# A two-layer attention block on one core: weighted values in three blocks a half instead of four

## The chip, the cores and the metric

The kernel runs on one NeuronCore of one Trainium2 chip. The metric is the device time of one execution in microseconds (us). The engines are named as in the profile: PE (TensorE, matmuls), DVE (VectorE), ACT (ScalarE), POOL (GpSimd) and SP (the queue that issues most transfers). PEld is the loading of weights into PE.

## What is computed

The input `x` is 8 images of 256 channels by 32 x 32 pixels, float32. Two attention layers follow each other; the second takes the first one's result. With `s = 1024` pixels and 8 heads of 32 channels, a layer is, cut to what matters:

```python
xn = group_norm(x, gamma, beta)                  # 32 groups of channels
qkv = einsum('bchw,oc->bohw', xn, w_qkv) + b_qkv
q, k, v = split(qkv per head)                    # 32 channels each
m = softmax(einsum('bhcs,bhct->bhst', q * scale, k * scale), axis=-1)
a = einsum('bhst,bhct->bhcs', m, v)
out = einsum('bchw,oc->bohw', a, w_proj) + b_proj
return x + out
```

## The kernel before, in words

The work is cut into 16 blocks (two layers of eight images), each into two groups of four heads. A block and a group are a **slot**; there are 32. In the code `s.g` is 0 for a block's first slot and 1 for its second. A slot has 64 **units** (`UNITS`), and falls into two **halves** of 32 units, one for each 512 queries. In a half there are 8 key tiles of 128 keys; unit `u` is one key tile and one of the four heads.

Every engine's program walks over the same units, in an order written out by numbers at the head of the file. In unit `u` PE does, in this order (`slot` of the PE program):

- `scores_t` (L398): 128 keys by 512 queries into one of three banks `ps_t`. ACT takes the exponential into a tile `pt` (L655).
- `dense` (L480, L488, L495): at two units of every eight, one part of a dense matmul into the single bank `ps_d`: queries and keys of two slots ahead (L480), values of the next block (L488), or the output projection of the block before (L495). Two parts make a step; its result is evacuated by ACT and DVE, or by DVE alone, one or two units later.
- `scores_for_max` (L425): scores with queries on the partitions, 40 units ahead, into one of three banks `ps_m`. DVE takes the row maxima (L737), and every eighth unit a small reduction over them (L746), which SP copies into row 96 of the queries.
- `sums` (L471): four matmuls with ones, once a half, that add up the exponentials of the half before over the partitions. They use a place in the ring of `ps_m`.
- `weighted_values` (L449): four matmuls of 32 columns for each key tile, side by side in the array, into `ps_v`.

What the ones-matmuls add up is made by POOL: `add` (L906) adds the key tiles of a half one by one, seven tiles in six additions of 128 x 2048, and `add_last_tile` (L913) starts a transfer that adds the eighth. `sums` waits for the landing:

```python
if t == ALL_BUT_LAST:
    pe.wait_ge(last_tile_added, 16 * (half + 1))
```

POOL's first addition of a half waits for the exponentials of its first two tiles, that is for unit 7. In the slots of group 0 POOL has `scale_and_shift` (L885 to L891) ahead of its additions: seven small operations on the statistics of the next block's group norm. They wait for `gm_done`, which ACT gives (L680) after PE's `group_stats` (L503). PE issues that at unit `GN_AT`. The next block's statistics are taken by DVE in the slots of group 1 (`channel_stats`, L771, at the units `STATS_AT`), and ACT normalises in the slots of group 0 at the units `NORMALISE_AT`.

When the sums of a half are there, DVE divides (`divide`: L784, L787, L790, L795). The attention result `att` of a half is what the output projection waits for. `values_out` (L663) copies `ps_v` away on ACT once the eighth tile of a half is in. A tile `pt` is one of six; an exponential waits until the tile six before it has been through `weighted_values` and through POOL's addition, or the transfer.

The last three halves are summed otherwise: POOL adds fewer tiles and PE's ones-matmuls take the rest, with no transfer.

## Time and profile before

| | us |
|---|---|
| median of 3 runs | 2068.94 (2068.49 to 2068.95) |
| the profiled execution | 2059.56 |
| its span | 2057.8 |
| PE busy | 2023.7 (98%) |
| POOL busy | 1838.2 (89%) |
| DVE busy | 1685.0 (82%) |
| ACT busy | 1248.9 (61%) |

The span is the time from the first to the last instruction in the profiled execution. Matmuls overlap in the pipeline, so PE's busy time says that it always had something, and the distance between starts is what a matmul costs. PE's granted clock is 0.997 of full speed on the mean. The run falls into a start of some 63 us, 32 slots, and an end of a few microseconds.

### The profile page before, as it was taken

The numbers are of one execution on the slowest core, as the hardware profiler recorded it, in microseconds if no ns is written. First come the engines' busy times: TensorE is split into PE (matmuls) and PEld (weight loads), VectorE is DVE, ScalarE is ACT, GpSimd is POOL, SyncE is SP. The second block draws the span as 40 slices with busy tenths as digits, with TensorE's granted clock in tenths as the row PEclk, the third lists the DMA queues.
The fourth block names the chain that finished last, engine by engine and source line by source line (L and its number), as shares of the span: only waits on it lengthen the run. The fifth ranks groups of instructions, "written<-read, shape, count | busy, mean of one in ns | idle before, by whom it ended". The sixth has DMA issues, their size and how long they took to land.

```text
span 2057.8 us, 30311 instructions
## 1 busy us (share of the span) xinstructions
PE 2023.7 (98%) x10080; PEld 1124.5 (55%) x10080; DVE 1685.0 (82%) x2896; ACT 1248.9 (61%) x2321; POOL 1838.2 (89%) x626
## 2 busy tenths in 40 slices
PE   6999999999999999999999999999999999999998
PEld 3455555655556555565555556555565555555543
DVE  5888888888888888888888888888888888888882
ACT  1556666666666666666566666666666666665664
POOL 2699999999899998999989999998999989999985
PEclk9999999999999999999999999999999999999999
DMA  4355455544456445366454555444564454654431
GB/s 129 73 112 105 92 113 124 119 104 96 107 110 144 100 90 120 83 143 144 102 107 86 123 124 121 106 94 109 107 144 103 88 118 85 143 123 83 105 60 42
DMA packets 217306, 220.31 MB, mean 107 GB/s; under 512 B 167488, under 2 KB 167616, under 8 KB 209344
## 3 DMA queue, kind: packets, MB, share of 16 engines
q1 hardware_dynamic: 207792, 152.84, 33.1%
q0 software_dynamic: 8784, 63.97, 15.9%
q10 hardware_dynamic: 576, 1.57, 0.4%
q8 instruction: 81, 1.33, 0.3%
q14 instruction: 73, 0.60, 0.1%
HBM read 36.32 MB, written 16.78 MB: 26 GB/s over the span
## 4 chain that ended last, share of the span: by engine, by line
PE 88%; DVE 6%; POOL 2%; DMA 2%; issue 1%; ACT 0%; SPq 0%; DVEq 0%; POOLq 0%; ACTq 0%
PE ps_t L398 23%; PE ps_m L425 21%; PE ps_v L449 20%; PE ps_d L480 10%; PE ps_d L495 5%; PE ps_d L488 5%; DVE raw_max L737 3%; PE ps_m L471 3%; POOL acc L906 2%; DMA acc<-pt 1%; DVE ps_m L790 1%; DVE att L795 1%; DVE turned L784 1%; DVE res L806 1%; PE ps_m L480 0%
## 5 line engine op out<-in xcount | busy, mean ns | idle before, releaser
L655 ACT ACTIVATE pt<-ps_t 128x512 f32<-128x512 f32 x2048 | 1122.1, 598 | 753.3 <-PE ps_t L398 728.6
L737 DVE TENSOR_REDUCE raw_max<-ps_m 128x1 f32<-128x512 f32 x2048 | 1332.5, 686 | 277.0 <-PE ps_m L425 275.3
L906 POOL TENSOR_TENSOR acc<-acc,pt 128x2048 f32<-128x2048 f32 x315 | 1442.4, 4579 | 45.1 <-ACT pt L655 1.4
L425 PE MATMUL ps_m<-ks,qs 96*128 96x512 f32 x2048 | 985.9, 482 | 8.3 <-DVE raw_max L737 6.0
L398 PE MATMUL ps_t<-qs,ks 97*128 97x512 f32 x2048 | 842.7, 413 | 1.3 <-ACT pt L655 1.1
L398 PEld LDWEIGHTS ps_t<-qs,ks 97*128 97x128 f32 x2048 | 389.5, 190 | 364.5 <-issue 216.1
L425 PEld LDWEIGHTS ps_m<-ks,qs 96*128 96x128 f32 x2048 | 388.6, 190 | 192.1 <-DVE raw_max L737 105.1
L449 PE MATMUL ps_v<-pt,v 128*32 128x512 f32 x4096 | 491.2, 597 | 0.0
L906 POOL TENSOR_TENSOR acc<-pt 128x2048 f32<-128x2048 f32 x64 | 300.3, 4692 | 61.4 <-ACT pt L655 60.3
L480 PE MATMUL ps_d<-xn,wq 128*128 128x512 f32 x500 | 256.9, 596 | 5.7 <-ACT xn L687 5.7
L449 PEld LDWEIGHTS ps_v<-pt,v 128*32 128x32 f32 x4096 | 113.9, 109 | 257.8 <-issue 187.4
L495 PE MATMUL ps_d<-att,wp 128*128 128x512 f32 x252 | 130.2, 597 | 4.7 <-DVE att L795 4.7
L488 PE MATMUL ps_d<-wq,xn 128*128 128x256 f32 x488 | 125.1, 378 | 0.0
L480 PEld LDWEIGHTS ps_d<-xn,wq 128*128 128x128 f32 x500 | 96.0, 192 | 30.1 <-issue 8.8
L488 PEld LDWEIGHTS ps_d<-wq,xn 128*128 128x128 f32 x488 | 92.2, 189 | 17.1
L913 POOL DMA_DIRECT2D acc<-pt x61 | 54.4, 892 | 34.1 <-ACT pt L655 33.6
L471 PE MATMUL ps_m<-acc,ones 128*32 128x512 f32 x512 | 68.1, 604 | 0.9 <-DMA acc<-pt 0.8
L784 DVE STREAM_TRANSPOSE turned<-ps_m 128x512 f32<-128x512 f32 x64 | 45.3, 708 | 27.7 <-PE ps_m L471 27.7
L495 PEld LDWEIGHTS ps_d<-att,wp 128*128 128x128 f32 x252 | 46.7, 190 | 21.5 <-issue 9.4
L674 ACT ACTIVATE stage_qh<-ps_d,par 128x512 fp32r<-128x512 f32 x63 | 43.0, 683 | 21.5 <-DMA ks<-stage_kh 13.8
L755 DVE SCALAR_TENSOR_TENSOR stage_ql<-ps_d,par,stage_qh 128x512 fp32r<-128x512 f32 x63 | 47.0, 746 | 9.5 <-ACT stage_qh L674 9.5
L806 DVE SCALAR_TENSOR_TENSOR res<-ps_d,bp,res 128x512 f32<-128x512 f32 x63 | 46.8, 743 | 9.2 <-PE ps_d L495 9.2
(50 smaller groups left out, 528.9 us busy)
## 6 DMA issues: line engine op xcount, KB each, us to landing
acc<-pt POOLq DMA_DIRECT2D x61, 1024.0 KB, 8.8
qs<-stage_qh SPq DMA_DIRECT2D x256, 128.0 KB, 2.4
ks<-stage_kh SPq DMA_DIRECT2D x248, 128.0 KB, 2.4
qs<-stage_ql SPq DMA_DIRECT2D x128, 128.0 KB, 2.5
qs<-neg_max SPq DMA_DIRECT2D x1024, 0.5 KB, 2.0
ks<-stage_kl SPq DMA_DIRECT2D x124, 128.0 KB, 2.4
xn<-x_dram SPq DMA_DIRECT2D x16, 512.0 KB, 4.5
res<-x_dram SPq DMA_DIRECT2D x16, 512.0 KB, 4.4
```

The source lines that it names most:

```text
L398: pe.matmul(ps_t[(UNITS * s.n + u) % RING][:, :], ks[s.qk][0:KROWS + 1, h, t * P:(t + 1) * P], qs[s.qk][0:KROWS + 1, h, hf * HALF:(hf + 1) ...
L425: pe.matmul(ps_m[place % RING][:, :], qs[b][0:KROWS, h, c:c + P], ks[b][0:KROWS, h, kf * HALF:(kf + 1) * HALF], start=True, stop=True).the ...
L449: mm = pe.matmul(ps_v[HD * h:HD * (h + 1), :], v[s.v][:, t, c:c + HD], tile_of(half, t)[:, h, :], start=(t == 0), stop=(t == NT - 1))
L471: mm = pe.matmul(ps_m[place % RING][HD * h:HD * (h + 1), :], ones[:, :], tile[:, h, :], start=first and k == 0, stop=last and k == len(til ...
L480: mm = pe.matmul(bank[:, :], wq[:, kt, c:c + P], xn[parity][:, kt, hf * HALF:(hf + 1) * HALF], start=(kt == 0), stop=(kt == CT - 1))
L488: mm = pe.matmul(bank[:, t * C:(t + 1) * C], xn[parity][:, kt, (2 * r + t) * P:(2 * r + t + 1) * P], wq[:, kt, 2 * C:3 * C], start=(kt == ...
L495: mm = pe.matmul(bank[:, :], wp[:, kt, ct * P:(ct + 1) * P], att[:, kt, hf * HALF:(hf + 1) * HALF], start=(kt == 0), stop=(kt == CT - 1))
L655: act.activation(tile_of(half, t)[:, h, :], ps_t[(UNITS * s.n + u) % RING][:, :], ACT.Exp, scale=SCALE).then_inc(exp_done, 1)
L737: dve.tensor_reduce(raw_max[:, e % 2, t, kf:kf + 1], ps_m[MAX_PLACE["max", UNITS * n + w] % RING][:, :], AX.X, ALU.max)\
L784: dve.transpose(turned[:, :], ps_m[bank][:, :]).then_inc(divide_step, 1)
L806: dve.scalar_tensor_tensor(out=r, in0=bank[:, :], scalar=bp[:, ct:ct + 1], in1=r, op0=ALU.add, op1=ALU.add).then_inc(proj_done, 1)
L906: pool.tensor_tensor(acc[hf][:, :, :], a[:, :, :], tile_of(half, t)[:, :, :], ALU.add).then_inc(pool_added, 1)
```

## The change

It sets the places anew at which things stand in a half. Only numbers and the code that reads them change.

- `weighted_values` stood at units 3, 11, 19 and 27 of a half, two key tiles each. Now it stands at unit 7 (the last two tiles of the half before), 17 (tiles 0 to 2) and 29 (tiles 3 to 5).
- A dense step's two parts stood three units apart, at the units 6 and 9 of every eight counted on (so 1, 6, 9, 14, 17, 22, 25 and 30 of a half). Now the four steps of a half stand at units 3 and 4, 11 and 16, 20 and 21, 26 and 27. No step reaches over into the next slot any more, so the code for that is gone.
- The ones-matmuls go from unit 19 to unit 17 of the next half, still ahead of the weighted values of that unit.
- The group statistics go from unit 7 to 9, the channel statistics from 39, 42, 44, 49 to 37, 39, 42, 44, the normalisation from 13, 17, 25, 29 to 17, 21, 25, 29, and `values_out` from unit 4 to unit 8.
- In the last three halves the sums go from unit 11 to 17, and the last slot's own places go up by one or two.

```diff
@@ -57,16 +57,17 @@
 LATER = 1
-PV_AT = 3
-PV_TILES = 2
-DENSE_AT = (6, 9)
-SUMS_AT = 19
-SUMS_AT_END = 11
+PV_BLOCKS = {7: (-2, -1), 17: (0, 1, 2), 29: (3, 4, 5)}
+LAST_TILES = 2
+VALUES_OUT_AT = 8
+DENSE_AT = ((3, 4), (11, 16), (20, 21), (26, 27))
+SUMS_AT = 17
+SUMS_AT_END = 17
 ROWS_AT = 7
 START_QK, START_LOW = 6, 2
-STATS_AT = (39, 42, 44, 49)
-GN_AT = 7
-NORMALISE_AT = (13, 17, 25, 29)
+STATS_AT = (37, 39, 42, 44)
+GN_AT = 9
+NORMALISE_AT = (17, 21, 25, 29)
...
 def dense_at(u, later=0):
 
-
-    v = u - later - DENSE_AT[0]
-    step, part = divmod(v, 2 * HG)
-    if part not in (0, DENSE_AT[1] - DENSE_AT[0]):
-        return None, None
-    return step, int(part > 0)
+    half, v = divmod(u - later, UNITS // NH)
+    for k, places in enumerate(DENSE_AT):
+        if v in places:
+            return len(DENSE_AT) * half + k, places.index(v)
+    return None, None
...
-                    if u % (PV_TILES * HG) == PV_AT:
-                        for done in range(u // HG - PV_TILES, u // HG):
-                            if done >= 0:
-                                weighted_values(s, done // NT, done % NT)
-                            elif not first:
-                                weighted_values(prev, NH - 1, NT + done)
+                    for tile in PV_BLOCKS.get(u % (UNITS // NH), ()):
+                        done = u // (UNITS // NH) * NT + tile
+                        if done >= 0:
+                            weighted_values(s, done // NT, done % NT)
+                        elif not first:
+                            weighted_values(prev, NH - 1, NT + done)
...
-LAST_OUT = 5
+LAST_OUT = 6
...
-LAST_SUMS_AT = 59
-LAST_KT0_AT = 60
+LAST_SUMS_AT = 61
+LAST_KT0_AT = 62
```

The order of the instructions shows the two places that matter most on PE, and one on DVE. The first is PE's queue in the second half of a slot of group 0, around the ones-matmuls (L471) of its first half. Before:

```order
L480 MATMUL ps_d<-xn1,wq 128x512
L425 MATMUL ps_m2<-ks1,qs1 128x512 [waits max_done]
L398 MATMUL ps_t1<-qs0,ks0 128x512 [waits exp_done]
L425 MATMUL ps_m0<-ks1,qs1 128x512 [waits max_done]
L398 MATMUL ps_t2<-qs0,ks0 128x512 [waits exp_done]
L425 MATMUL ps_m1<-ks1,qs1 128x512 [waits max_done]
L471 MATMUL ps_m2<-acc0,ones 32x512 [waits last_tile_added,max_done]
L471 MATMUL ps_m2<-acc0,ones 32x512 x3
L449 MATMUL ps_v<-pt0,v0 32x512 [waits exp_done]
L449 MATMUL ps_v<-pt0,v0 32x512 x3
L449 MATMUL ps_v<-pt1,v0 32x512 [waits exp_done]
L449 MATMUL ps_v<-pt1,v0 32x512 x3
```

and now:

```order
L480 MATMUL ps_d<-xn1,wq 128x512
L425 MATMUL ps_m1<-ks1,qs1 128x512 [waits max_done,staged_head3]
L398 MATMUL ps_t0<-qs0,ks0 128x512 [waits exp_done]
L425 MATMUL ps_m2<-ks1,qs1 128x512 [waits max_done]
L471 MATMUL ps_m0<-acc0,ones 32x512 [waits last_tile_added,max_done]
L471 MATMUL ps_m0<-acc0,ones 32x512 x3
L449 MATMUL ps_v<-pt4,v0 32x512 [waits raw_done,exp_done]
L449 MATMUL ps_v<-pt4,v0 32x512 x3
L449 MATMUL ps_v<-pt5,v0 32x512 [waits exp_done]
L449 MATMUL ps_v<-pt5,v0 32x512 x3
L449 MATMUL ps_v<-pt0,v0 32x512 [waits exp_done]
L449 MATMUL ps_v<-pt0,v0 32x512 x3
```

The four ones-matmuls stand two units sooner, and three tiles of weighted values, which begin their half, stand behind them where there were two from its middle. Their first matmul waits for the transfer (`last_tile_added`), and with it all that follows.

The second place is PE's queue around the group statistics, in the first half of a slot of group 0. Before:

```order
L398 MATMUL ps_t2<-qs0,ks0 128x512 [waits exp_done]
L495 MATMUL ps_d<-att,wp 128x512 [waits norm_done,qkl_done]
L425 MATMUL ps_m0<-ks0,qs0 128x512 [waits max_done]
L398 MATMUL ps_t0<-qs0,ks0 128x512 [waits exp_done]
L425 MATMUL ps_m1<-ks0,qs0 128x512 [waits max_done]
L503 MATMUL ps_v<-channel_mv,group 128x4 [waits mv_summed,raw_done]
```

and now:

```order
L449 MATMUL ps_v<-pt1,v1 32x512 [waits exp_done]
L449 MATMUL ps_v<-pt1,v1 32x512 x3
L398 MATMUL ps_t1<-qs0,ks0 128x512 [waits exp_done]
L425 MATMUL ps_m2<-ks0,qs0 128x512 [waits max_done]
L398 MATMUL ps_t2<-qs0,ks0 128x512 [waits exp_done]
L425 MATMUL ps_m0<-ks0,qs0 128x512 [waits max_done]
L503 MATMUL ps_v<-channel_mv,group 128x4 [waits mv_summed,raw_done]
```

L503 stood four units behind the weighted values at unit 3; now it stands two units behind those at unit 7.

The third place is DVE's queue in the first half of a slot of group 1, around the division (L784 to L795 before, L778 to L789 now; L763 or L757 evacuates values, L737 or L731 takes the maxima). Before:

```order
L737 TENSOR_REDUCE raw_max<-ps_m 128x1 x2
L763 TENSOR_TENSOR v<-ps_d,bv 128x512
L737 TENSOR_REDUCE raw_max<-ps_m 128x1 x2
L784 STREAM_TRANSPOSE turned<-ps_m 128x512
L787 RECIPROCAL rden<-turned 128x16
L790 STREAM_TRANSPOSE ps_m<-rden 128x512
L795 TENSOR_TENSOR att<-raw,ps_m 128x512
L737 TENSOR_REDUCE raw_max<-ps_m 128x1 x4
L746 TENSOR_REDUCE neg_max<-raw_max 128x4
L737 TENSOR_REDUCE raw_max<-ps_m 128x1 x2
L763 TENSOR_TENSOR v<-ps_d,bv 128x512
```

and now:

```order
L731 TENSOR_REDUCE raw_max<-ps_m 128x1
L757 TENSOR_TENSOR v<-ps_d,bv 128x512
L731 TENSOR_REDUCE raw_max<-ps_m 128x1
L778 STREAM_TRANSPOSE turned<-ps_m 128x512
L781 RECIPROCAL rden<-turned 128x16
L784 STREAM_TRANSPOSE ps_m<-rden 128x512
L789 TENSOR_TENSOR att<-raw,ps_m 128x512
L731 TENSOR_REDUCE raw_max<-ps_m 128x1 x4
L757 TENSOR_TENSOR v<-ps_d,bv 128x512
L731 TENSOR_REDUCE raw_max<-ps_m 128x1 x2
L740 TENSOR_REDUCE neg_max<-raw_max 128x4
```

The evacuation behind the division comes after four maxima instead of six, with the next one eight maxima behind it.

## Rows read from the trace of the kernel before

**Rows 1.** The page: the span, and busy time by engine.

```profile
span 2057.8 us, 30311 instructions
PE 2023.7 (98%) x10080; PEld 1124.5 (55%) x10080; DVE 1685.0 (82%) x2896; ACT 1248.9 (61%) x2321; POOL 1838.2 (89%) x626
```

**Rows 2.** Chain of waits, 1040 to 1200 us: start us, us, what.

```profile
1110.95 0.61 ACT pt L655
1111.60 4.59 POOL acc L906
...
1125.68 0.48 issue
1126.17 10.32 DMA acc<-pt
1136.62 1.07 PE ps_m L471 x8
```

**Rows 3.** All 61 transfers of line 913: who waited, us, times; and landing.

```profile
  PE ps_m L471: 0.8, 3
...
DMA to landing us min/median/max: 7.2/8.8/10.9
```

**Rows 4.** Chain of waits, 1000 to 1035 us.

```profile
1007.07 0.23 PE ps_t L398
1007.30 0.86 PE ps_d L488 x4
1008.17 0.23 PE ps_m L425
...
1010.43 0.24 PE ps_m L425
...
1011.60 0.99 PE ps_m L471 x8
1012.60 1.72 PE ps_v L449 x16
```

**Rows 5.** Timeline of PE, 1003.5 to 1006.5 us: start us, us, engine, line, operation.

```profile
1003.68 0.39 PE L425 MATMUL ps_m<-ks,qs 96*128 96x512 f32 x1
1004.00 1.92 PE L449 MATMUL ps_v<-pt,v 128*32 128x512 f32 x16
1005.86 0.50 PE L398 MATMUL ps_t<-qs,ks 97*128 97x512 f32 x1
1006.20 0.40 PE L425 MATMUL ps_m<-ks,qs 96*128 96x512 f32 x1
```

**Rows 6.** Timeline of PE, 1055 to 1064 us; a slot of group 0 begins at 1055.99.

```profile
1055.99 0.40 PE L398 MATMUL ps_t<-qs,ks 97*128 97x512 f32 x1
...
1063.50 0.28 PE L503 MATMUL ps_v<-channel_mv,group 128*128 128x4 f32 x2
```

**Rows 7.** Timeline of POOL, its statistics and transfers, with idle time before and releaser.

```profile
128.60 0.89 POOL L913 DMA_DIRECT2D acc<-pt  x1 [0.55 <-ACT pt L655]
...
190.59 0.18 POOL L885 TENSOR_TENSOR sq<-gm 128x2 f32<-128x2 f32 x1 [1.28 <-ACT gm L680]
...
315.46 0.18 POOL L885 TENSOR_TENSOR sq<-gm 128x2 f32<-128x2 f32 x1 [2.04 <-ACT gm L680]
346.64 0.93 POOL L913 DMA_DIRECT2D acc<-pt  x1 [0.55 <-ACT pt L655]
...
1064.99 0.18 POOL L885 TENSOR_TENSOR sq<-gm 128x2 f32<-128x2 f32 x1 [2.04 <-ACT gm L680]
1096.45 0.93 POOL L913 DMA_DIRECT2D acc<-pt  x1 [0.55 <-ACT pt L655]
1126.17 0.87 POOL L913 DMA_DIRECT2D acc<-pt  x1 [0.55 <-ACT pt L655]
...
1814.52 0.18 POOL L885 TENSOR_TENSOR sq<-gm 128x2 f32<-128x2 f32 x1 [2.04 <-ACT gm L680]
```

**Rows 8.** Timeline of DVE, 1013 to 1018 us: a division and four maxima.

```profile
1013.11 0.71 DVE L784 STREAM_TRANSPOSE turned<-ps_m 128x512 f32<-128x512 f32 x1
...
1015.57 2.54 DVE L737 TENSOR_REDUCE raw_max<-ps_m 128x1 f32<-128x512 f32 x4
```

More of the change, by code:

```diff
@@ L510, in dense @@
                     return
-                if step < 0:
-                    if has_next and not first:
-                        project_qk(1 - s.g, s.v if s.g == 0 else 1 - s.v, 3, part)
-                    return
                 r = step % 4
@@ L626, in _ @@
             last = plain(SLOTS - 1)
-            for t in range(NT - PV_TILES, NT):
+            for t in range(NT - LAST_TILES, NT):
                 sums(HALVES - 1, (t,), first=False, last=t == NT - 1)
@@ L692, in slot @@
                     exp(s, u)
-                    if u == PV_AT + LATER and not first:
+                    if u == VALUES_OUT_AT and not first:
                         values_out(NH * s.n - 1)
-                    if u == PV_AT + LATER + UNITS // NH:
+                    if u == VALUES_OUT_AT + UNITS // NH:
                         values_out(NH * s.n)
@@ L701, in slot @@
                     step, part = dense_at(u, LATER)
-                    if part == 1 and step < 0 and has_next and not first:
-                        qk_high(s.n + 1, 1 - s.g, s.v if s.g == 0 else 1 - s.v, 3)
                     if part == 1 and step >= 4 and has_second:
@@ L819, in slot @@
                     step, part = dense_at(u, 2 * LATER)
-                    if part == 1 and step < 0 and has_next and not first:
-                        qk_low(s.n + 1, 1 - s.g, s.v if s.g == 0 else 1 - s.v, 3)
                     if part == 1 and step >= 4 and has_second:
```

## The prediction

> **What bounds the kernel now.** I read the totals first, then the chain of waits, then TensorE's timeline, then POOL's. The totals show TensorE busy for 98% of the span [rows 1], so a microsecond saved or lost in its queue is one of the whole. The chain of waits is TensorE nearly throughout, but around 1111 to 1137 us it leaves it: an exponential releases POOL's additions, these release the transfer that adds the eighth key tile, 10.32 us from issue to landing, and that releases the ones-matmul L471 [rows 2]. So POOL's chain ends last at that one place, and elsewhere just misses: in the whole run L471 waited for the transfer 3 times, 0.8 us together [rows 3]. The two chains are level, and anything that makes TensorE come to L471 sooner will meet a wait.
>
> **Prices on TensorE.** Word for word: a unit is one L398 and one L425, 0.2345 us each, 0.469 together (0.23 and 0.24 in the chain); a dense part is 0.86; the four ones-matmuls are 0.86 plus 0.13 for going in; two key tiles of weighted values are 1.72, so one is 0.86 [rows 4]. From L425 at 1003.68 to L425 at 1006.20 is 2.52 us [rows 5]; less two matmuls of 0.235 that is 2.05, so a visit to the 32-column matmuls costs 0.33 beside its 1.72. A half before: 32 x 0.469 + 8 x 0.86 values + 0.86 sums + 8 x 0.86 dense + 4 x 0.33 = 30.97 us.
>
> **What the change takes away.** Four visits a half become three (the sums still share one). That is 0.33 x 64 halves = 21 us, and a half becomes 30.64. The dense matmuls are as many; they cost the same wherever they stand, since L425 after one starts without any gap.
>
> **What it moves.** Call H the start of a slot of group 0. Group statistics (L503) stood 7.51 us behind H [rows 6]: 8 units, 2 dense parts, one visit (3.75 + 1.73 + 2.05 = 7.53). Now 10 units, 2 parts, one visit: 8.47. The sums stood at unit 19 of a half: 20 units, 5 parts, 2 visits = 17.8. Now unit 17: 18 units, 4 parts, one visit = 8.44 + 3.45 + 2.05 = 13.94. So TensorE reaches the sums 3.9 us sooner, and what they wait for starts 0.96 later. What is queued behind this wait is everything: three tiles of weighted values, then all scores; VectorE and ScalarE run dry.
>
> **POOL's chain, from rows 7.** The statistics reach POOL 1.49 us behind L503 (1064.99 against 1063.50), so 9.96 after H now. From there to the issue of the transfer of the slot's first half 31.18 (346.64 - 315.46, a round without a hitch); from that issue to the next half's 29.72. This is POOL's own work, nothing of it changes. Landing takes 7.2 to 10.9, median 8.8 [rows 3]; in the first half of a slot, where the SP queue copies the staged heads at the same time, the chain row shows 10.32. The transfer that matters lands in such a half: I take 9.6, between the median and that row.
>
> First half of the slot: issue at H + 41.1, landing about H + 49.5; due at H + 30.64 + 13.94 = 44.6. TensorE waits some 4 to 5 us (less 1.4 if it waited in the half before). Second half: issue at H + 70.8, landing at H + 80.4; after the first wait TensorE is due at about the same time, 80 to 80.4. Then 16.7 us remain of that half (30.64 - 13.94), and 30.64 of the next, and the next H stands at 9.96 + 31.18 + 29.7 + 9.6 + 16.7 + 30.64 = **127.8 us**. The other two sums of a round: the third lands early enough; the fourth (its first addition waits for unit 7's exponential, 6.1 us into the half now) comes some 1.4 late, which lies beside POOL's wait for the next statistics.
>
> Onto this go TensorE's waits for VectorE. VectorE takes 0.62 us a maximum (2.54 for four in a row) and 2.46 for a division (from 1013.11 to 1015.57) [rows 8], TensorE gives one every 0.47, and three banks lie between. Before, dense parts stood 3 and 5 units apart; now units 22 to 25 stand without one, behind an evacuation of 0.6 at unit 22: the fourth of them finds its bank taken, about 0.6 us, in the halves whose dense results VectorE evacuates at once. In the half with the channel statistics (four more operations of 0.6 at units 5 to 12) some 0.6 at units 14 and 15 and 0.4 at the sums. On the path that is 1.5 a round; its bounds are 0 (TensorE was late anyway) and 3.0. Round after: **129.3**.
>
> Round before: from POOL's first row of the statistics at 190.59 to that at 1814.52 are 13 rounds, 124.92 each [rows 7]; that is 4 x 30.97 plus 1.0 of such waits. The difference is +4.4, over the 14 rounds up to the last two slots: +61.6. The first two slots have no statistics in their way, POOL is back to back: second transfer issued at 128.60, landing near 137.6, and 0.1 + 16.7 + 0.6 + 30.64 + 1.0 behind it is H = 186.6; before it was 190.59 - 9.0 = 181.6 (9.0 from H to POOL's row of the statistics, 1064.99 - 1055.99): +5. The last two slots: one late sum of 1.4, less three visits, bounds -1 and +3: +1. **Sum: +67 us**, against the profiled execution's 2059.56 (span 2057.8): 2126.6. The runs' median is 9.4 us above it, 2068.94; I add the same 67: 2136.
>
> A rule to weigh: the rows show 7.2 us as the fastest landing of 61. The Trainium skill (DMA: Bandwidth & Descriptors, Anatomy of one DMA — SWDGE path) gives 2.0 us plus bytes over 436 GB/s, an estimate of 4.4 us for this 1 MB. By that page the waits would nearly vanish, and the round would be about 125.6, the time some 2079. The trace disagrees at every one of its transfers, and stands.
>
> **Rivals.**
> - **Only the visits count (faster).** The place is L471; the mechanism is a landing, or a POOL chain, early enough that it never waits. It decides at H + 44.6: the transfer would have to land 3.5 us after its issue at 41.1. Then -21 for the visits, +8 for half a microsecond of bank waits a round: 2056. For it: the 0.33 is real [rows 5]. Against it: no landing under 7.2 [rows 3]. The Trainium skill (TensorEngine Tiling, Key Properties) says that a change of tiling mode drains the engine, and by that alone the change gains; the 0.33 agrees. Chance 0.06.
> - **The transfers land quicker (7.4).** They are issued earlier in their half, so may miss the staged copies. Then the first half's landing rules: H + 48.5 + 0.1 + 16.7 + 13.94 = 79.3 at the second sum, round 128.2, +3.3 x 14 + 6 = 52: 2121. Chance 0.17.
> - **VectorE's waits are larger.** 3.0 a round and landings of 10.6 give 131.8, +6.9 x 14 + 7 = 104: 2173. For it: VectorE is 82% busy [rows 1], and the even spacing of its work is what the change gives up. Chance 0.12.
> - **The moves don't bite** (a stall of VectorE or ScalarE elsewhere was already hiding them, so TensorE comes to the sums no earlier): within 0.2%, 2069. Against it: TensorE's rows stand end to end before L471. Chance 0.03.
>
> **How the numbers follow.** The forecast, 2123 to 2158, has 0.62. Time 2136. The range reaches down into the quick landings, 2112, and up to landings of 10.3 with waits of 2.2 (130.7 a round, +81 + 6 = 87: 2156), so 2158. A measurement of this kernel can tell about 0.2% (4 us) from no change. Faster: 0.07 (the first rival and some of what I don't see). Same: 0.03. Slower: 0.90.
>
> **What would show it.** L471 waiting for the transfer in nearly every half of group 0, by 3 to 5 us at the first and up to 2 at the second, and some 1.4 in the first half of each slot of group 0, 60 to 100 us in all; rounds of 128 to 130.5 between POOL's statistics rows; POOL's wait for the statistics grown from 2.04 to 4 us or more; TensorE's share of the chain down to about half, POOL's and the transfer's up to about half; bank waits at unit 25. It is wrong if L471 shows no such wait, if the round is under 126, or if the additions are not 4.7 us apart any more.

## The result, and the profile after

| | before | after |
|---|---|---|
| median us | 2068.72 (2059.67 to 2068.95, 4 runs) | 2202.48 (2199.05 to 2206.81, 4 runs) |
| profiled execution us | 2059.56 | 2206.81 |
| mean of 13 rounds (one block: two slots, four halves; from one first row of POOL's statistics to the next) us | 124.92 | 134.26 |

After over before is 1.066 (95% interval 1.0644 to 1.0676): 6.6% slower. The sign was forecast; the time, 2136 with a range of 2112 to 2158, was not. The loss is twice the 67 us of the forecast.

The page of the changed kernel, its totals and its chain by engine and line, answers to [rows 1]:

```profile
span 2205.0 us, 30311 instructions
PE 2069.4 (94%) x10080; PEld 1131.1 (51%) x10080; DVE 1677.3 (76%) x2896; ACT 1247.8 (57%) x2321; POOL 1834.6 (83%) x626
...
PE 38%; POOL 19%; SPq 17%; DMA 11%; DVE 7%; issue 4%; ACT 4%; POOLq 0%; ACTq 0%; DVEq 0%
POOL acc L898 18%; PE ps_v L449 11%; SPq L295 10%; PE ps_t L398 8%; DMA acc<-pt 8%; PE ps_m L425 7%; SPq L305 6%; PE ps_d L480 5%; DVE raw_max L731 5%; DMA qs<-stage_ql 3%; PE ps_m L471 3%; ACT pt L651 2%; PE ps_d L495 2%; DVE stats L765 1%; PE ps_d L488 1%
```

The instructions are the same in number, and every engine is idle for a larger share. TensorE carried 88% of the chain before and now 38%. POOL with its transfer (L898, `acc<-pt`: 26%) was expected there. What was not is SP's queue: its copies of staged heads (L295) and of rows (L305), and the landing of the last of them, are another 19%. The waits, engine, line and releaser with us in total, times, longest, say the same; the first answers to [rows 3], the third to the idle times in [rows 7]:

```profile
PE ps_m L471 <- DMA acc<-pt: 62.2, 30, 4.8
ACT stage_qh L670 <- DMA qs<-stage_ql: 34.6, 20, 9.3
POOL sq L877 <- ACT gm L676: 85.6, 16, 8.8
PEld ps_m L425 <- DVE raw_max L731: 145.8, 429, 1.1
```

The last of them was 105.1 us in 384 times before, so VectorE holds TensorE up more too.

POOL's first and last row of the statistics, 13 rounds apart, answer to [rows 7]:

```profile
207.47 0.18 POOL L877 TENSOR_TENSOR sq<-gm 128x2 f32<-128x2 f32 x1 [5.30 <-ACT gm L676]
1952.81 0.18 POOL L877 TENSOR_TENSOR sq<-gm 128x2 f32<-128x2 f32 x1 [5.35 <-ACT gm L676]
```

Twelve rounds lie between 132.2 and 135.7 us; one, at the change of layer, is 141.9. The 147.2 us between the two spans are 121.4 in these 13 rounds, 16.9 ahead of the first row and 8.9 behind the last. Some 6 of the 16.9 are in the start, where the same code ran at a lower granted clock (0.66 to 0.83 between 30 and 70 us, where it was 1.00 up to 60 us before); no run settles where that came from.

The chain between 1096 and 1152 us (start, us, what) shows both chains outside TensorE, one behind the other, and answers to [rows 2]:

```profile
1100.48 0.59 SPq L295
...
1101.11 5.24 DMA qs<-stage_ql
...
1106.53 0.69 ACT stage_qh L670
1107.22 0.98 ACT pt L651 x2
...
1108.28 4.57 POOL acc L898
...
1137.52 11.10 DMA acc<-pt
...
1148.76 1.06 PE ps_m L471 x8
1149.82 2.58 PE ps_v L449 x24
```

From a slot's start on SP issues the copies of the next slot's four heads: six transfers (L295) and four rows (L305) for each head, at 0.60 us an issue. ScalarE's `qk_high` (L670) overwrites the staged tile for the slot after that, and waits until all of these copies have landed. Exponentials stand behind L670 in ScalarE's queue, and POOL's additions behind those.

The ones-matmuls of the same round, in TensorE's timeline (start, us, operation, idle before and releaser), show where the 134 us are spent. With the first of them, at 1050.47, shown further down, they are the four sums of a round:

```profile
1083.02 1.07 PE L471 MATMUL ps_m<-acc,ones 128*32 128x512 f32 x8
1116.01 1.06 PE L471 MATMUL ps_m<-acc,ones 128*32 128x512 f32 x8
1148.76 1.06 PE L471 MATMUL ps_m<-acc,ones 128*32 128x512 f32 x8 [0.59 <-DMA acc<-pt]
```

On the mean of the 13 rounds the first sum comes 39.6 us behind POOL's row, with 3.2 us of waiting, and the next ones 32.9, 34.1 and 32.7 us later, where TensorE's own work in a half is 30.64. The second sum waited in four of the 13 rounds (1.6 to 1.9 us), the third in none. So less than half of the loss is TensorE standing at L471.

### The profile page after: what moved, and what is told of

It reads as the page before. It is cut to its first block, busy times and chain, and to the rows that moved or that the text cites. A ratio compares the mean times of both kernels' runs of the same rounds, so it can differ in the third digit from the quotient of the medians.

```text
span 2205.0 us, 30311 instructions
## 1 busy us (share of the span) xinstructions
PE 2069.4 (94%) x10080; PEld 1131.1 (51%) x10080; DVE 1677.3 (76%) x2896; ACT 1247.8 (57%) x2321; POOL 1834.6 (83%) x626
## 4 chain that ended last, share of the span: by engine, by line
PE 38%; POOL 19%; SPq 17%; DMA 11%; DVE 7%; issue 4%; ACT 4%; POOLq 0%; ACTq 0%; DVEq 0%
POOL acc L898 18%; PE ps_v L449 11%; SPq L295 10%; PE ps_t L398 8%; DMA acc<-pt 8%; PE ps_m L425 7%; SPq L305 6%; PE ps_d L480 5%; DVE raw_max L731 5%; DMA qs<-stage_ql 3%; PE ps_m L471 3%; ACT pt L651 2%; PE ps_d L495 2%; DVE stats L765 1%; PE ps_d L488 1%
## 5 line engine op out<-in xcount | busy, mean ns | idle before, releaser
L731 DVE TENSOR_REDUCE raw_max<-ps_m 128x1 f32<-128x512 f32 x2048 | 1309.8, 685 | 330.2 <-PE ps_m L425 329.1
L898 POOL TENSOR_TENSOR acc<-acc,pt 128x2048 f32<-128x2048 f32 x315 | 1439.9, 4571 | 55.6 <-ACT pt L651 13.8
L425 PE MATMUL ps_m<-ks,qs 96*128 96x512 f32 x2048 | 995.1, 487 | 27.8 <-DVE raw_max L731 25.2
L425 PEld LDWEIGHTS ps_m<-ks,qs 96*128 96x128 f32 x2048 | 389.3, 190 | 268.8 <-DVE raw_max L731 145.8
L898 POOL TENSOR_TENSOR acc<-pt 128x2048 f32<-128x2048 f32 x64 | 297.1, 4642 | 148.7 <-ACT pt L651 147.6
L449 PEld LDWEIGHTS ps_v<-pt,v 128*32 128x32 f32 x4096 | 129.7, 113 | 287.0 <-issue 260.1
L480 PE MATMUL ps_d<-xn,wq 128*128 128x512 f32 x500 | 265.2, 614 | 5.7 <-ACT xn L683 5.7
L471 PE MATMUL ps_m<-acc,ones 128*32 128x512 f32 x512 | 74.2, 651 | 64.9 <-DMA acc<-pt 62.2
L495 PE MATMUL ps_d<-att,wp 128*128 128x512 f32 x252 | 128.9, 592 | 1.8 <-DVE att L789 1.8
L778 DVE STREAM_TRANSPOSE turned<-ps_m 128x512 f32<-128x512 f32 x64 | 45.6, 712 | 102.4 <-PE ps_m L471 102.2
L480 PEld LDWEIGHTS ps_d<-xn,wq 128*128 128x128 f32 x500 | 95.2, 195 | 32.6 <-issue 10.6
L670 ACT ACTIVATE stage_qh<-ps_d,par 128x512 fp32r<-128x512 f32 x63 | 43.1, 684 | 59.6 <-DMA qs<-stage_ql 34.6
L877 POOL TENSOR_TENSOR sq<-gm 128x2 f32<-128x2 f32 x16 | 3.0, 185 | 85.6 <-ACT gm L676 85.6
L471 PEld LDWEIGHTS ps_m<-acc,ones 128*32 128x32 f32 x512 | 11.5, 110 | 90.4 <-issue 63.7
```

The lines of the kernel that those rows point to most:

```text
L425: pe.matmul(ps_m[place % RING][:, :], qs[b][0:KROWS, h, c:c + P], ks[b][0:KROWS, h, kf * HALF:(kf + 1) * HALF], start=True, stop=True).the ...
L449: mm = pe.matmul(ps_v[HD * h:HD * (h + 1), :], v[s.v][:, t, c:c + HD], tile_of(half, t)[:, h, :], start=(t == 0), stop=(t == NT - 1))
L471: mm = pe.matmul(ps_m[place % RING][HD * h:HD * (h + 1), :], ones[:, :], tile[:, h, :], start=first and k == 0, stop=last and k == len(til ...
L480: mm = pe.matmul(bank[:, :], wq[:, kt, c:c + P], xn[parity][:, kt, hf * HALF:(hf + 1) * HALF], start=(kt == 0), stop=(kt == CT - 1))
L495: mm = pe.matmul(bank[:, :], wp[:, kt, ct * P:(ct + 1) * P], att[:, kt, hf * HALF:(hf + 1) * HALF], start=(kt == 0), stop=(kt == CT - 1))
L731: dve.tensor_reduce(raw_max[:, e % 2, t, kf:kf + 1], ps_m[MAX_PLACE["max", UNITS * n + w] % RING][:, :], AX.X, ALU.max)\
```

## The experiments

The texts on what was expected were written before each run. "Round" is the mean between POOL's rows of the statistics, and TensorE's own work in a round is 4 x 30.64 = 122.6 us by the prediction's prices. Where the ones-matmuls stand at unit 19 beside the three blocks, they are a fourth visit of their own, and it is 4 x 30.97 = 123.9. "Waits" below is a round less this own work: a remainder, in which the granted clock is included. The kernel before ran again beside each group of kernels, with medians of 2062.9 to 2068.7 us; each ratio is to its own group's.

**All staged copies at the slot's start.**

```diff
-                    if has_next and u < HG * MAX_GROUP:
-                        stage_head(s.n + 1, 1 - s.qk, u // MAX_GROUP)
+                    if has_next and u == 0:
+                        for h in range(HG):
+                            stage_head(s.n + 1, 1 - s.qk, h)
```

> The changed kernel, with the copies of all four staged heads issued at a slot's start instead of one every eight units; nothing else. Theory A (two chains take turns: POOL's additions and their transfer up to the second sum of a round, and SP's queue of staged copies behind it, which the evacuation of the first dense step of a second half, moved from unit 41 to 37, waits for): the wait for the staged copies goes, the round falls from some 133.7 us to about 129.5, and the extra 9 us at the change of layer go too, so about 2202 - 14 x 4 - 9 = 2137; the waits of the ones-matmuls for the transfer stay. Theory B (SP's queue alone sets the round, and the waits for the transfer only fill what it leaves): close to the kernel before, 2070 to 2090. Theory C (the forecast's mechanism alone, with TensorE's clock falling in the waits as what it left out): no change beyond 5 us, 2202.

Measured: 2211.32, ratio 1.072 (1.069 to 1.0757). The wait of L670 for these copies is gone, but the rows of the maxima stand behind them in the same queue now:

```profile
PE ps_t L399 <- DMA qs<-neg_max: 45.5, 31, 2.6
PE ps_m L472 <- DMA acc<-pt: 30.9, 21, 3.7
```

The wait moved to another user of SP's queue; the loss stayed.

**Weighted values ahead of the ones-matmuls in unit 17** (their two pieces of code change places).

> The changed kernel, with the weighted values of unit 17 ahead of the ones-matmuls instead of behind them. TensorE then has 2.6 us of work of its own in front of the wait. Theory A: the waits at the ones-matmuls shrink by 2.6 us each and TensorE's clock no longer falls there (1.4 us in about half the rounds), 3 to 4 us a round, 2202 - 50 = about 2150; the wait for the staged copies stays. Theory B: no change beyond 5 us. Theory C: 2202 - 14 x 4 to 6 = 2120 to 2145.

Measured: 2251.59, ratio 1.0926 (1.0891 to 1.096). L471 hardly waits any more (1.1 us in 2 times), but the division now starts behind the block of values with nothing of length behind it: L480 waits for VectorE's evacuation 60.0 us in 30 times, L495 for `att` 23.8. In the changed kernel the block of three covers the division.

**POOL's first addition ahead of its seven small operations.**

```diff
-                if s.g == 0 and has_second and not first:
-                    scale_and_shift(s.j + 1, 1 - s.v)
                 for hf in range(NH):
                     for t in range(1, pooled_in(NH * s.n + hf)):
                         add(NH * s.n + hf, hf, t)
+                        if s.g == 0 and has_second and not first and hf == 0 and t == 1:
+                            scale_and_shift(s.j + 1, 1 - s.v)
```

> The changed kernel, with POOL's seven small operations on the statistics behind its first addition of the half instead of ahead of it, so that the additions no longer wait for the statistics (5.3 us a round). Theory A: POOL's chain gets 3.8 us shorter, the first wait of a round for the transfer falls by that, and the round by 3 to 4 us: about 2150. Theory B: no change beyond 5 us, since SP's queue sets the round. Theory C: 2202 - 14 x 4 to 5 = 2130 to 2145.

Measured: 2148.60, ratio 1.0403 (1.0364 to 1.0442), round 129.8. One order on an engine that is not even busy gives 54 us back: POOL no longer waits for the late statistics (85.6 us to 12.0), and L471 waits 31.8 instead of 62.2. The two chains are shorter here, but not gone: SP's queue still has 20% of the chain and POOL 19%, and L670 waits for the staged copies 21.3 us.

**The three edits together.**

> The changed kernel with all three edits: heads staged early, weighted values ahead of the ones-matmuls, POOL's statistics behind its first addition. Theories A and B: no chain reaches TensorE any more, a half is 30.64 us and TensorE waits for VectorE only, some 2 us a round: 4 x 30.64 + 2 = 124.6 a round, about the kernel before, 2060 to 2075. Theory C: the same. If it stays above 2090, something else in the new places costs.

Measured: 2262.26, ratio 1.0961 (1.0932 to 1.099), no better than values_first alone. L481 waits for VectorE's evacuation 59.9 us in 30 times, as there, so the exposed division is still in the way.

**In the second half of a slot, the first dense step at units 6 and 8 instead of 3 and 4, and the second at 12 and 16 instead of 11 and 16.**

```diff
-DENSE_AT = ((3, 4), (11, 16), (20, 21), (26, 27))
+DENSE_AT = (((3, 4), (11, 16), (20, 21), (26, 27)), ((6, 8), (12, 16), (20, 21), (26, 27)))
```

> The changed kernel, with the first two dense steps of a second half four units later (units 6 and 8, 12 and 16 instead of 3 and 4, 11 and 16), so that the evacuation that waits for the staged copies comes at unit 41 of the slot, as in the kernel before, instead of 37. Theory A (POOL's chain with its transfer sets the two halves of a slot of group 0, SP's queue of staged copies and rows the second half of a slot of group 1; heads_early only traded one wait on that queue for another): the waits of ScalarE for the staged copies (34.6 us, 20 times) go, 3.4 us a round and the 9 us at the change of layer, 2202 - 48 - 9 = 2145. Theory C (the copies' queue costs nothing, all is POOL's chain and the clock): 2202 within 5.

Measured: 2184.92, ratio 1.0583 (1.0555 to 1.0612), round 132.8. The staged wait is gone and so is the long round at the change of layer. It gives only 1.5 us a round: it has a cost of its own (L480 waits for `stage_ql` 19.6 us), and POOL's chain, beside it, now ends last (L471 waits 49.4, POOL for the statistics 107.4). The mean granted clock is 0.992 here and 0.980 in the change, so a part of the 1.5, which no run takes out, may be the clock's.

**The ones-matmuls at unit 19 again** (`SUMS_AT = 19`).

> The changed kernel with one number undone: the ones-matmuls back at unit 19. They are a visit of their own then, 0.33 us a half, and stand 3.9 us later in TensorE's work, where the kernel before has them. Theory A: the waits for the transfer shrink from 2.6 to 4.8 us to under 1, the clock does not fall, the round gets 3.5 to 4.5 shorter; against that the output projection at unit 20 waits for the division, 2.8 us in one half of four, beside POOL's chain: 2145 to 2165. If the place of the sums was not the cause: 2202 + 20 for the visits.

Measured: 2205.53, ratio 1.0696 (1.0671 to 1.0721), no clear difference from the change, although the fourth visit alone is 21 us by its price. The waits at L471 vanish; the staged copies take their place (35.3 us in 15 times), and L495 waits for `att` 36.9.

**No transfers: the ones-matmuls take the eighth key tile too.**

```diff
-                                sums(half, (ALL_BUT_LAST,))
+                                sums(half, (POOLED, POOLED_TILES))
...
-                    if NH * s.n + hf < END:
-                        add_last_tile(NH * s.n + hf, hf)
```

> The changed kernel without the transfer: the eighth key tile goes into the ones-matmuls itself, four more of them a half, 0.86 us. All is still computed. The sums then wait for POOL's sixth addition alone, about H + 40.6, and are due at H + 44.6: no wait. Theory A: a half is 31.5, with 2.1 a round of waits for VectorE 128.1, and 0 to 3 for the staged copies, which no longer share the queues with the transfer: 2202 - 14 x 4 = about 2145, between 2125 and 2165. If the landing was not what TensorE waited for: 2202 + 55 for the four matmuls.

Measured: 2141.01, ratio 1.0383 (1.0347 to 1.0419), round 130.1: 61 us faster than the change although TensorE has 0.86 us more in each half. Its own work is 126.0 a round, so 4.1 are waits; TensorE has 81% of the chain, VectorE 10% and ScalarE 3%, and L668 waits for the staged copies 3.8 us in all, so these are waits for banks nearly alone. The issue of head 0's copies in SP's queue (start, us) shows what else the transfer does. In the changed kernel, with a transfer of POOL's issued at 1071.77:

```profile
1072.73 0.57 SPq L295 DMA_DIRECT2D ks<-stage_kh  x1
...
1076.44 3.18 SPq L295 DMA_DIRECT2D qs<-stage_qh  x2
1079.67 0.61 SPq L295 DMA_DIRECT2D qs<-stage_ql  x1
```

and without transfers:

```profile
1035.71 0.57 SPq L295 DMA_DIRECT2D ks<-stage_kh  x1
...
1037.88 1.14 SPq L295 DMA_DIRECT2D qs<-stage_qh  x2
1039.07 0.58 SPq L295 DMA_DIRECT2D qs<-stage_ql  x1
```

The six take 7.6 us against 4.0. In the changed kernel 32 of the 124 groups of six overlap one of POOL's transfers, and take 3.8 to 9.7 us, 7.3 in the middle; the others take 3.7 to 5.2. In the kernel before, where the transfers are issued at other points of these groups, the overlapping ones take 3.7 to 5.8. So the removal of the transfer acts on both chains, and its 61 us are not the price of the wait at L471 alone.

**POOL's order and the later dense steps together.**

> The changed kernel with both: the first dense steps of a second half later, and POOL's statistics behind its first addition (which alone gave 2148.6). Theory A: the two add up, since one shortens POOL's part of the path and the other SP's: round 129.9 - 3.4 = 126.5, 2148.6 - 48 - 4 = 2097, between 2085 and 2110. If pool_order had already moved the path off the copies' queue: 2145.

Measured: 2146.40, ratio 1.0402 (1.0381 to 1.0422), round 130.0 (129.0 to 129.2 in eleven, 136.8 and 134.3 at the change of layer). L471 waits 6.6 us in 3 times, and the staged copies 5.1 in 2. Both chains are all but off the path (POOL has 3% of the chain, SP 2%), and the kernel is still 4% slower than before: 129.0 in the ordinary rounds is 6.4 over TensorE's own work. Of that some 1.6 a round belong to the later steps (L480 waits for `stage_ql` 24.9 us in 30 times). So a third loss was left, and the next runs ask whether it is TensorE's waits for banks.

**The three blocks alone, in the kernel before** (dense parts, ones-matmuls and channel statistics at their old units).

```diff
-PV_AT = 3
-PV_TILES = 2
+PV_BLOCKS = {7: (-2, -1), 17: (0, 1, 2), 29: (3, 4, 5)}
 DENSE_AT = (6, 9)
 SUMS_AT = 19
-GN_AT = 7
-NORMALISE_AT = (13, 17, 25, 29)
+GN_AT = 9
+NORMALISE_AT = (17, 21, 25, 29)
```

> The kernel before with the three blocks of weighted values alone (units 7, 17, 29; values_out at 8, group statistics at 9, normalisation at 17 to 29, the end's places as in the change), and the dense parts, the ones-matmuls (unit 19) and the channel statistics where they were. Theory A, the loss lies in the new places of the dense work, in two ways (maxima of VectorE bunched, and the evacuation of the first query/key step ahead of SP's staged copies): a half costs TensorE 30.64 as in my ledger, a round about 123.6 to 124.5 (124.9 before), no staged-copy wait, L471 waiting for the transfer by up to 10 us in all; time 2050 to 2066, not slower than before. Theory B, the blocks themselves bring the loss (three tiles in a row let the rings of scores run dry): round 127 or more, time 2095 or more.

Measured: 2243.77, ratio 1.0873 (1.085 to 1.0895), round 136.7 (136.5 to 138.1), with no wait at L471 or for the staged copies among the larger ones. Theory A of that text fell: the blocks bring the loss. Its half of 30.64 was a slip as well, since the ones-matmuls at unit 19 are a fourth visit here; against 123.9 the waits are 12.8. In the kernel before, the profile lists 13 waits of these matmuls for a maximum, 6.0 us, all in the start; here L426 waits for VectorE's maxima 39.6 us in 106 times, and for `att` 35.4 in 47. VectorE in its turn waits longer for scores: 446.2 us in 375 times, at most 3.0, where it was 275.3 in 559, at most 1.3. Rows of TensorE's and VectorE's timeline (start, us, operation, idle before) show one part of it, the division bare behind the ones-matmuls:

```profile
1035.37 1.06 PE L472 MATMUL ps_m<-acc,ones 128*32 128x512 f32 x8
...
1036.50 0.72 DVE L785 STREAM_TRANSPOSE turned<-ps_m 128x512 f32<-128x512 f32 x1 [0.21 <-PE ps_m L472]
...
1037.26 0.25 DVE L788 RECIPROCAL rden<-turned 128x16 f32<-128x16 f32 x1
...
1037.54 0.73 DVE L791 STREAM_TRANSPOSE ps_m<-rden 128x512 f32<-128x512 f32 x1
...
1038.38 0.69 DVE L796 TENSOR_TENSOR att<-raw,ps_m 128x512 f32<-128x512 f32 x1
...
1039.21 1.10 PE L496 MATMUL ps_d<-att,wp 128*128 128x512 f32 x2 [1.39 <-DVE att L796]
```

**The same with POOL's order changed.**

> blocks_only, and POOL does its first addition of the slot ahead of the seven small operations on the group statistics. By theory A POOL's chain has a microsecond or more of slack and the rounds are TensorE's own 122.6 plus a microsecond of bank waits, 123.6: time 2045 to 2056, the fastest so far. By theory B as blocks_only.

Measured: 2247.55, ratio 1.0882 (1.0856 to 1.0908), round 136.6: nothing, since POOL's chain is not on this path.

**The same without transfers.**

> blocks_only without the transfers: the ones-matmuls take the eighth key tile themselves, 0.86 us more a half, so that only TensorE's own work and its waits for VectorE's and ScalarE's banks are left. The same edit on the changed kernel gave rounds of 130.1 (126.0 and 4.1 of bank waits). Theory A: here 126.0 plus about 1, so 127.0, and the bank waits of the changed kernel come from its dense places; time about 2095 to 2105. Theory B: 129.5 or more, as there.

Measured: 2283.73, ratio 1.1056 (1.1024 to 1.1089), round 138.9. Its own work is 127.3 (four visits and 0.86 more a half), not the 126.0 of that text, so 11.5 are waits: for banks, and for the bare division.

**The kernel before with POOL's order changed.**

> The kernel before, with POOL's first addition ahead of its seven small operations and nothing else. There POOL's chain and TensorE are level (L471 waits 3 times, 0.8 us), so I expect no difference: 2064 to 2070, rounds 124.5 to 124.9. If the order of POOL's work were a gain in itself, apart from the changed kernel's waits (the rival), it would be 2040 or less.

Measured: 2073.75, ratio 1.0042 (1.0028 to 1.0057), round 125.7. The edit that gives the changed kernel 54 us costs this one 9. In its trace the exponentials wait for POOL's additions 53.4 us instead of 16.4, and the normalisation for `gn_c` 16.0 instead of 2.5. It pays only where the statistics come late.

**Maxima over 256 of 512 columns**, in the blocks alone, in the change without transfers, in the change, and in the kernel before. These four leave half of the keys out of the maxima, and scale the exponent down so that it stays finite; they don't compute the layer's result, and only show what quicker maxima are worth. An exponential takes 0.60 us in them as in the others.

```diff
-ps_m[MAX_PLACE["max", UNITS * n + w] % RING][:, :],
+ps_m[MAX_PLACE["max", UNITS * n + w] % RING][:, 0:HALF // 2],
...
-ACT.Exp, scale=SCALE)
+ACT.Exp, scale=SCALE / 64)
```

> blocks_only, with every maximum of VectorE over 256 of its 512 columns (half of the keys are left out of the maxima, and the exponent is scaled down so that it stays finite; all other work as before). Theory V: the 12 us a round that blocks_only loses are waits of TensorE for VectorE: three tiles of weighted values (2.7 us) leave VectorE without maxima, and it is not quick enough to make that up behind three banks. Then quicker maxima bring the round near TensorE's own 122.6: 123 to 125.5, time 2045 to 2080, and the waits for raw_max nearly vanish. Rival S: the rings of the exponentials or the evacuations of ps_d are what runs dry; then the round stays at 132 or more.

> The changed kernel without transfers (ones_tile), with the same halved maxima. Its rounds were 130.1 against 126.0 of TensorE's own work. Theory V: the 4.1 are waits for VectorE's maxima and its other work behind them; with halved maxima 126.0 to 127.2, time 2085 to 2105. Rival S: 129 or more.

> The changed kernel with the same halved maxima, and with its transfers. If the two chains outside VectorE (POOL's with its transfer, SP's staged copies) hold the round by themselves, it stays at 131 or more and the waits at L471 grow beyond 62 us: time 2165 or more. If the waits for VectorE are a term that adds up with them, the round falls by about 4, to 130, time about 2150. If everything hung on VectorE it would be 124, 2065.

> The kernel before with the same halved maxima: the control. Its rounds are 124.9 with 123.9 of TensorE's own work, so at most 1 us a round can come back: 2048 to 2068, if POOL's chain allows it; rounds of 123.9 to 124.9.

| with halved maxima | us | ratio to before | round | round with whole maxima |
|---|---|---|---|---|
| blocks alone | 2160.08 | 1.0468 (1.0428 to 1.0508) | 131.7 | 136.7 |
| change, no transfers | 2100.27 | 1.0172 (1.014 to 1.0203) | 127.9 | 130.1 |
| change | 2166.79 | 1.0493 (1.0419 to 1.0567) | 132.6 | 134.3 |
| before | 2046.05 | 0.9907 (0.9866 to 0.9948) | 124.3 | 124.9 |

The groups of the maxima in the blocks-alone kernel, whole and halved (busy, mean ns, idle before):

```profile
L738 DVE TENSOR_REDUCE raw_max<-ps_m 128x1 f32<-128x512 f32 x2048 | 1312.4, 684 | 454.7 <-PE ps_m L426 446.2
```

```profile
L738 DVE TENSOR_REDUCE raw_max<-ps_m 128x1 f32<-128x256 f32 x2048 | 817.7, 421 | 808.2 <-PE ps_m L426 788.7
```

Quicker maxima give back 5.0 us a round beside long blocks and 0.6 beside short ones; L426's waits for a maximum fall from 39.6 us to 3.7. So the waits are VectorE's to a good part (theory V), yet not wholly: 131.7 is no 125.5. About half of the 7.8 left over 123.9 is the division behind the ones-matmuls (L426 and L496 still wait for `att` 59.5 us, 3.7 a round); the chain goes through ScalarE for another 6%, and through SP and its landings for 4%. In the changed kernel the quicker maxima are worth 1.7, with waits at L471 grown to 75.5 us, and 2.2 of the 4.1 where the transfers are away. No run settles what the other 1.9 are; the kernel before has 1.0 of such a remainder.

**The blocks, with the ones-matmuls at unit 17 and the old dense places; then with POOL's order changed too.**

```diff
-SUMS_AT = 19
+SUMS_AT = 17
```

> blocks_only with the ones-matmuls at unit 17 instead of 19, so that three tiles of weighted values stand between them and the next scores. In blocks_only the division (2.5 us) lay bare behind them: the timeline shows two scores, then TensorE waiting for att. Theory C: this is most of the 11.7 us a round; here the cover is there, the division's waits (raw for L426 and L496 on att, 156 us of PE and PEld together) vanish, and what is left is VectorE's and ScalarE's bank waits under the old dense places and L471's waits for the transfer: rounds of 128 to 131, time 2110 to 2155, faster than the change. Rival D, the old dense places are what doesn't go with long blocks: rounds of 133.5 or more, 2190 or more.

> blocks_sums17 with POOL's first addition ahead of its seven small operations, which takes POOL's chain back by some 2 us or more in group 0. Theory C: the waits at L471 shrink to under 15 us, and the rounds show the old dense places with long blocks by themselves: 126 to 129, time 2085 to 2125, below pool_dense (129.0, 2146), so the new dense places cost as well. Rival D: 131 or more, above pool_dense, so the new dense places are a gain beside the long blocks.

Measured: 2172.98, ratio 1.0539 (1.0505 to 1.0574), round 131.9; and 2150.95, ratio 1.042 (1.0385 to 1.0455), round 130.0. The ones-matmuls ahead of the block of three are worth 71 us. By its price the visit saved is 21 of them, and most of the rest is the covered division: the waits for `att` at L426 and L496 fall from 60.0 us to 5.0. Neither theory of those two texts is right: with POOL's order changed, rounds of 130.0 with the old dense places stand beside ordinary rounds of 129.0 with the later ones (pool_dense), and two long rounds there bring the means level. The chain of the last kernel shows the form of the wait that is left:

```profile
1048.81 0.25 PE ps_m L426
1049.07 0.02 issue
1049.09 0.69 DVE raw_max L738
1049.78 0.60 DVE v L764
1050.38 0.61 DVE raw_max L738
1050.98 0.04 issue
1051.03 0.50 PE ps_m L426
```

An evacuation of 0.60 stands between two maxima, shortly behind a block, and TensorE comes with scores every 0.47 us. No version here that computes the layer beats the kernel before.

## Why the prediction was wrong

**Right: the transfer at L471, and POOL waiting longer.** L471 waits 62.2 us in all, within the 60 to 100 forecast, at most 4.8 a time. POOL waits 5.3 us for the statistics (4 or more forecast). pool_order and ones_tile take the wait's two ends away and give back 54 and 61 us. The total is in part luck: nine of the 15 waits at a first sum are under the 3 us forecast as the least, and the second sum waits only now and then.

**Right: visits.** The changed kernel's timeline of TensorE has the price again, around a block of three with no wait:

```profile
1064.90 0.39 PE L425 MATMUL ps_m<-ks,qs 96*128 96x512 f32 x1
1065.22 2.78 PE L449 MATMUL ps_v<-pt,v 128*32 128x512 f32 x24
1067.93 0.50 PE L398 MATMUL ps_t<-qs,ks 97*128 97x512 f32 x1
1068.27 0.40 PE L425 MATMUL ps_m<-ks,qs 96*128 96x512 f32 x1
```

From L425 to L425 are 3.37 us; less two matmuls of 0.235 and three tiles of 0.86 that is 0.32. It is a gain of 1.3 a round, which no run shows by itself, and it stays under every loss.

**Wrong: the term for bank waits.** The step was "On the path that is 1.5 a round; its bounds are 0 (TensorE was late anyway) and 3.0." The term is 4.1 in ones_tile, and 6.4 in pool_dense's ordinary rounds, 1.6 of it by its own later steps; blocks17_pool, with the old dense places, has 7.4. The stall that I had worked out is there: 30 waits of L425 for a maximum, 11.1 us together, some 9 us behind L471, at unit 25. I had gone unit by unit through the dense parts, and left out that the block itself starves VectorE: for 2.6 us it gets no scores, and it has three banks to live on. It is idle then (its mean wait for scores grows from 0.49 us to 1.19 in blocks_only, where the ones-matmuls don't wait), and what it loses it can't make up between blocks, where scores come every 0.47 us and a maximum takes 0.62. Before, its gap was 1.7 us every 7.7. The rival "VectorE's waits are larger" had the right cause with 3.0, still too little. That VectorE's maxima are a part of it is shown by the halved ones; that the block's length does it is argued from that and from blocks_only, where nothing but the blocks and their followers moved.

**Wrong: what TensorE does behind the first wait.** The step was "after the first wait TensorE is due at about the same time, 80 to 80.4", which set POOL's second transfer on the path, and counted 16.7 + 30.64 behind it with no loss of their own. The first sum came as forecast, 39.6 us behind POOL's row against 39.5. The second came 32.9 later where 30.9 were forecast, so that in nine of 13 rounds TensorE itself was later than the transfer; and from there to the next row of POOL's are 61.8 us against 57.3. These 2.0 and 4.5, less the 1.5 forecast for bank waits on top, are the whole difference between 129.3 and 134.3. That POOL's chain sets the whole round was wrong; it sets the first sum.

**Wrong: a queue left out.** The step was "What it moves." It follows L503 and the ones-matmuls, and passes over the first dense step of a slot's second half, whose parts came from units 38 and 41 to 35 and 36. Its evacuation, five units sooner, waits for SP's copies of the staged heads. In the trace of before the issues of such a slot end at 1154.42, and the evacuation stands at 1159.98 without a wait, so they had landed by then. In the changed kernel the wait is 34.6 us in 20 times; dense_later removes it for 1.5 us a round, and the longest, 9.3 us, makes the round of 141.9 at the change of layer. The forecast had nothing for it.

**Wrong: how the terms join.** I set one chain of 127.8 and laid 1.5 on it. The runs show chains that take turns: with both chains all but away a round is 130.0 (pool_dense), with POOL's chain 132.8 (dense_later), with SP's copies too 134.3. Taken off one at a time from the other side they are worth 54 us (POOL's order), 18 (dense steps) and -9 (early copies), which adds up to nothing simple. In the one order, the round before of 124.9 loses 1.3 by the visits, and gains 6.4 (130.0 against 122.6, less the 1.0 before), 2.8 (POOL and transfer) and 1.5 (SP), sum 9.4, where 134.3 - 124.9 = 9.4. In the other order POOL's order takes off 4.5 and the dense steps nothing more (129.8 and 130.0), so the split is one way of counting and not a measurement of each. In the forecast a round lost 4.4, nearly all of it to POOL and the transfer.

**A term left out: the clock.** The mean granted clock is 0.980 of full speed, against 0.997 before. As an estimate from these two, 1.7% of 2205 us is 37 us, or 2.3 a round; it is an upper bound, since a low clock costs nothing while TensorE waits. Pool_order, pool_dense and ones_tile have 0.993 to 0.998, so that a part of what they give back is the clock's; no run takes it apart from the waits that bring it on.

**The test in the text** said rounds of 128 to 130.5; they are 134.3. The chain was to be half TensorE and half POOL and the transfer; it is 38% and 27% (POOL 19%, its transfer 8%), and more than half of the rest is SP's queue and its landings. Outside the 13 rounds the loss is 25.8 us, where some 10 were forecast (5 and 1, and 4.4 for a fourteenth round); 6 of the difference are the slower start.

## What to carry to other kernels

Gathering work on the busiest engine saves its mode changes (0.33 us a visit here), but an engine that it feeds through a few banks can go idle for the length of the gathered block. Price that block by what the next busiest engine (82% here) loses in it and can't make up, before pricing what it saves. For each step that moves earlier, list all that its evacuation waits for, transfers of another queue too, and ask how late they were before. When a change makes several chains late, removing one wait says little: build the version with all of them gone, check in its chain that they are, and read the floor from that.

## What was not expected of the hardware

**The clock falls in a wait.** At the change of layer TensorE waits for the staged copies, and the chain shows its work behind that wait:

```profile
1237.52 9.71 DMA qs<-stage_ql
...
1247.42 0.69 ACT stage_qh L670
...
1250.34 0.43 PE ps_t L398
...
1251.62 1.71 PE ps_d L480 x2
...
1255.25 0.23 PE ps_t L398
...
1256.43 0.86 PE ps_d L480 x2
```

A score matmul takes 0.43 and a dense part 1.71, twice the 0.23 and 0.86 of a few microseconds later and of [rows 4]: the lower of the two levels, 1.2 instead of 2.4 GHz. Short waits at L471 can do it too. The timeline of TensorE around one (start, us, operation, idle before and releaser), and the windows there (us, busy PE, PEld, DVE, ACT, POOL, granted clock, DMA share, GB/s):

```profile
1050.47 1.94 PE L471 MATMUL ps_m<-acc,ones 128*32 128x512 f32 x8 [2.55 <-DMA acc<-pt]
1052.15 3.43 PE L449 MATMUL ps_v<-pt,v 128*32 128x512 f32 x24
```

```profile
1045.00:1050.00 5.00, 2.93 (x11) 1.63 (x9) 3.74 (x7) 3.32 (x7) 4.86 (x2) 1.00 0.79 143
1050.00:1052.00 2.00, 1.53 (x8) 0.46 (x12) 0.00 (x0) 0.00 (x0) 2.00 (x1) 0.52 0.11 9
1052.00:1056.00 4.00, 4.00 (x30) 1.31 (x23) 3.05 (x5) 0.00 (x0) 3.86 (x2) 0.81 0.00 0
```

After an idle time of 2.55 us the granted clock is 0.52, and the ones-matmuls with the block of three take some 1.5 us longer. Not every wait does it: none of the 16 at L471 up to 1.90 us was followed by slower ones-matmuls (1.06 us), and of the 15 of 2.45 to 4.79 us ten were (1.17 to 1.94 us) and five weren't, one of 2.88 among them. The forecast had no such term. The Trainium skill (TensorE: Matmul & The Clock Gate, Loop structure matters more than you think) asks that TensorE not be left idle while transfers land; the rows agree.

**A transfer slows another queue's issues, by where it starts.** Head 0's six copies took 7.6 us just behind the issue of an accumulating transfer of POOL's, and 4.0 without one. Six that began 6.3 us behind such an issue, at 1011.15, with the transfer still in flight, took 4.3. The Trainium skill (DMA: Bandwidth & Descriptors, SWDGE vs HWDGE vs iDMA) says that POOL's and SP's transfers feed different queues inside each DMA engine, which the engine serves in turn; these numbers agree that the two share something, but the page says nothing on the time of an issue, and no run takes the sharing apart.
